# A bank for the value product of the second cross-attention, and the experts' constants and six tiles' gates made before their stage

## The reference

```python
x = x + L0_xattn(ctx, layernorm(x), mask)      # cross-attention, rms-normed heads
x = x + L0_attn(layernorm(x))
x = x + L0_ffn(layernorm(x))                   # small gated low-rank experts
x = x + L1_xattn(layernorm(x), ctx)            # 16 heads of 32, softmax over 257 context rows
x = x + L1_attn(layernorm(x))                  # product of two rotary score matrices, causal
x = x + L1_ffn(layernorm(x))                   # 8 experts of 1024, the best 2 for each token
```

## Time and profile before

| | us |
|---|---|
| median of three timed executions | 1955.49 |
| lowest and highest of them | 1949.67, 1959.02 |
| the profiled execution | 1950.19 |
| its span, first to last instruction | 1948.5 |
| PE busy | 1635.4 (84%) |
| DVE busy | 1301.4 (67%) |
| ACT busy | 957.0 (49%) |
| POOL busy | 616.8 (32%) |

### The profile page before, as it was taken

How to read it: one execution, slowest core, us unless ns; L and a number is a source line. 1 busy time by engine, 2 the same in 40 slices (tenths; PEclk the granted TensorE clock), 3 DMA queues, 4 the chain that set the end, 5 groups by cost and what they waited for, 6 DMA issues and landing times. The chain is left out here.

```text
span 1948.5 us, 43594 instructions
## 1 busy us (share of the span) xinstructions
PE 1635.4 (84%) x15542; PEld 1112.1 (57%) x15542; DVE 1301.4 (67%) x2926; ACT 957.0 (49%) x2169; POOL 616.8 (32%) x730
## 2 busy tenths in 40 slices
PE   6959999999976888399889889759996189989996
PEld 3525555555544666366666666525554077777775
DVE  7858888888855777367777777667775654454441
ACT  5635656565544344255565565533333255565551
POOL 4544545454522110111111111025544123333332
PEclk9989999999987999699999999979998589999998
DMA  5111101011130000101011001330000475665512
GB/s 192 50 49 31 41 30 41 30 41 30 33 124 12 1 2 2 56 27 33 25 32 33 26 31 33 133 133 29 12 12 12 152 223 146 164 186 157 143 31 67
DMA packets 50064, 126.86 MB, mean 65 GB/s; under 512 B 6913, under 2 KB 19425, under 8 KB 49889
## 3 DMA queue, kind: packets, MB, share of 16 engines
q1 hardware_dynamic: 44914, 113.10, 17.9%
q0 software_dynamic: 5008, 11.80, 3.1%
HBM read 111.29 MB, written 15.68 MB: 65 GB/s over the span
## 5 line engine op out<-in xcount | busy, mean ns | idle before, releaser
L106 PE MATMUL e_pGU<-XT,WB 128*128 128x128 f16 x1344 | 233.3, 222 | 18.9 <-issue 9.6
L107 PE MATMUL e_pGU<-XT,WB 128*128 128x128 f16 x1344 | 233.2, 222 | 0.0
L108 PE MATMUL e_pGU<-XT,WB 128*128 128x128 f16 x1344 | 233.2, 222 | 0.0
L2506 DVE SCALAR_TENSOR_TENSOR WB<-w5in,WB 128x1024 f16<-128x1024 f32 x96 | 115.5, 1223 | 85.9 <-ACT WB L2649 85.9
L1639 POOL TENSOR_TENSOR dLT<-dx,dLT 128x768 f16<-128x768 f32 x32 | 52.7, 1647 | 356.6 <-DVE dLT L1663 356.6
L106 PEld LDWEIGHTS e_pGU<-XT,WB 128*128 128x128 f16 x1344 | 134.0, 100 | 24.4 <-issue 22.8
L107 PEld LDWEIGHTS e_pGU<-XT,WB 128*128 128x128 f16 x1344 | 134.0, 100 | 1.5
L108 PEld LDWEIGHTS e_pGU<-XT,WB 128*128 128x128 f16 x1344 | 134.1, 100 | 0.0
L106 PE MATMUL dpK<-dLT,W 128*128 128x256 f16 x384 | 105.9, 276 | 19.0 <-POOL dLT L1639 19.0
L2489 POOL TENSOR_TENSOR XT<-e_mf,XT 128x256 f16<-128x256 f32 x84 | 56.2, 670 | 174.1 <-ACT XT L2663 174.1
L706 POOL TENSOR_TENSOR crn<-css,mhalf 128x8 f32<-128x8 f32 x64 | 106.6, 1666 | 5.3
(11 more groups left out here) (517 smaller groups left out, 5610.4 us busy)
## 6 DMA issues: line engine op xcount, KB each, us to landing
w5in<-in_WE SPq DMA_DIRECT2D x96, 512.0 KB, 4.7
cx<-in_ctx SPq DMA_DIRECT2D x32, 384.0 KB, 3.1
dx<-in_ctxT SPq DMA_DIRECT2D x32, 384.0 KB
w5in<-in_W SPq DMA_DIRECT2D x14, 512.0 KB, 8.6
wpiece<-in_W SPq DMA_DIRECT2D x12, 512.0 KB, 9.3
w3in<-in_W SPq DMA_DIRECT2D x11, 512.0 KB, 9.0
v<-vlat SPq DMA_DIRECT2D x32, 96.0 KB
X<-in_x SPq DMA_DIRECT2D x8, 256.0 KB, 8.2
```

Source lines behind the costliest of these rows:

```text
L106: pe.matmul(out, lh, rh, start=first, stop=False, skip_group_check=shared)
L107: pe.matmul(out, lh, rl, start=False, stop=False, skip_group_check=shared)
L108: return pe.matmul(out, ll, rh, start=False, stop=last, skip_group_check=shared)
L2506: dve.scalar_tensor_tensor(WB[w][:, 1, a], ring[n][:, :], WS, WB[w][:, 0, a], ALU.mult, ALU.subtract)\
```

## The change

It has two parts.

In **cross1** the first half of a batch's values goes into the bank `dpO`, the second into `dpV` (`pVs`). The waits of `values` and `outputs` are rewritten for that. The low half of XT, `out_low`, moves from DVE to POOL, with a new wait of `out_sum` for it. ACT reads the turned probabilities before it gathers the queries.

In **poly** POOL makes the experts' constants at the end of slot 3, SP loads 128 token numbers instead of 1024 and the partition's own number at the start of the stage, and at the end of slot 8 DVE makes the gates of the first six tiles (`EARLY` = 6), with an exponential on ACT. The experts' head makes the gates of the last two tiles, has no constants to make and no numbers to load, and computes its bounds from `count` a little later.

The core of the diff (left out: the declarations of the tiles that now live in both stages, and renamings that follow from them):

```diff
--- before.py
+++ after.py
@@ -1585,6 +1589,7 @@
         pV, pO, pS = ps("dpV", [P, D]), ps("dpO", [P, G, P]), ps("dpS", [P, G, 512])
+        pVs = (pO[:, :, :].rearrange("p g n -> p (g n)"), pV[:, :])
@@ -1643,12 +1648,21 @@
+            def out_low(b):
+                pool.wait_ge(sig["d_ohi"], b + 1)
+                sig.passed(pool, "pool")
+                dst = XT[:, :, :, ds(b * S, S)]
+                pool.tensor_tensor(dst[:, 1, :, :], zo[:, :, :], dst[:, 0, :, :], ALU.subtract).then_inc(sig["d_olo"], 1)
+
...
                     low(b + 1, 1 - u)
-
-            walk(pool, body, lambda: low(0, 0))
+                if prev:
+                    out_low(b - 1)
+
+            sig.begin(pool, "d_olo")
+            walk(pool, body, lambda: low(0, 0), lambda: out_low(B - 1))
@@ -1672,7 +1686,7 @@
                 dve.wait_ge(sig["d_vhi"], q + 1)
-                dve.scalar_tensor_tensor(vb[u][:, i, 1, :], pV[:, :], 1.0 / WS, vb[u][:, i, 0, :], ALU.mult, ALU.subtract)\
+                dve.scalar_tensor_tensor(vb[u][:, i, 1, :], pVs[i], 1.0 / WS, vb[u][:, i, 0, :], ALU.mult, ALU.subtract)\
@@ -1702,16 +1716,12 @@
                 dve.wait_ge(sig["d_o"], b + 1)
+                dve.wait_ge(sig["d_olo"], b + STARTS["d_olo"])
...
                        .then_inc(sig["d_z"], 1)
-
-            def out_low(b):
-                dve.wait_ge(sig["d_ohi"], b + 1)
-                dst = XT[:, :, :, ds(b * S, S)]
-                dve.tensor_tensor(dst[:, 1, :, :], zo[:, :, :], dst[:, 0, :, :], ALU.subtract).then_inc(sig["d_olo"], 1)
@@ -1765,7 +1773,7 @@
                 act.wait_ge(sig["d_v"], q + 1)
-                act.activation(vb[u][:, i, 0, :], pV[:, :], ACT.Copy, scale=1.0 / WS).then_inc(sig["d_vhi"], 1)
+                act.activation(vb[u][:, i, 0, :], pVs[i], ACT.Copy, scale=1.0 / WS).then_inc(sig["d_vhi"], 1)
@@ -1798,10 +1806,11 @@
                 value_high(2 * b, u, 0)
-                gather(b, u)
...
                     probs_high(b - 1, 1)
+                sig.passed(act, "act")
+                gather(b, u)
@@ -1830,10 +1839,15 @@
-            def values(q, u, i):
-                pe.wait_ge(sig["d_vlo"], q + STARTS["d_vlo"])
+            def values(b, u, i):
+                if i == 0:
+                    if not isinstance(b, int) or b:
+                        pe.wait_ge(sig["d_vlo"], 2 * b - 1 + STARTS["d_vlo"])
+                        pe.wait_ge(sig["d_z"], BPT * b - BPT + STARTS["d_z"])
+                else:
+                    pe.wait_ge(sig["d_vlo"], 2 * b + STARTS["d_vlo"])
                 for k in range(XK):
-                    m = product(pe, pV[:, :], hl(LT[u], k, slice(i * P, (i + 1) * P)), hl(Wv, k), k == 0, k == XK - 1)
+                    m = product(pe, pVs[i], hl(LT[u], k, slice(i * P, (i + 1) * P)), hl(Wv, k), k == 0, k == XK - 1)
@@ -1856,9 +1870,8 @@
-            def outputs(b, u):
-                pe.wait_ge(sig["d_vlo"], 2 * b + 2 + STARTS["d_vlo"])
-                pe.wait_ge(sig["d_z"], BPT * b + STARTS["d_z"])
+            def outputs(b, u, nxt=1):
+                pe.wait_ge(sig["d_vlo"], 2 * b + 2 + nxt + STARTS["d_vlo"])
@@ -1876,17 +1889,18 @@
                 keys(b, u)
-                values(2 * b, u, 0)
+                values(b, u, 0)
...
                     turn_probs(b - 1)
-                values(2 * b + 1, u, 1)
+                values(b, u, 1)
...
                 turn_probs(B - 1)
-                outputs(B - 1, (B - 1) % 2)
+                pe.wait_ge(sig["d_z"], BPT * (B - 1) + STARTS["d_z"])
+                outputs(B - 1, (B - 1) % 2, 0)
@@ -2024,6 +2046,17 @@
                     pattern_low(3, q)
+                if s == 3:
+                    tri, before16, ones16 = st["tri"], st["before16"], st["ones16"]
+                    pool.memset(tri[:, :, :], 1.0).then_inc(sig["p_made"], 1)
+                    pool.memset(before16[:, :], 1.0).then_inc(sig["p_made"], 1)
+                    pool.memset(ones16[:, :], 1.0).then_inc(sig["p_made"], 1)
+                    pool.tensor_copy(st["ident16"][:, :], ident[:, :]).then_inc(sig["p_made"], 1)
+                    pool.wait_ge(sig["p_made"], 4)
+                    pool.affine_select(out=tri[:, :, :], in_=tri[:, :, :], compare_op=ALU.is_gt, fill=0.0, base=0,
+                                       pattern=[[1, 8], [-1, 8]], channel_multiplier=0).then_inc(sig["p_made"], 1)
+                    pool.affine_select(out=before16[:, :], in_=before16[:, :], compare_op=ALU.is_gt, fill=0.0, base=0,
+                                       pattern=[[1, P]], channel_multiplier=-1).then_inc(sig["p_made"], 1)
@@ -2148,6 +2181,13 @@
                     logits(r)
+                if r == EARLY - 1:
+                    dve.wait_ge(sig["p_lgc"], EARLY)
+                    dve.wait_ge(sig["p_made"], 6)
+                    for m in (0, 2):
+                        dve.wait_ge(sig[f"p_rr{m}"], NT)
+                    gates(sig, dve, "p_g", 0, LG[:, few, :], st["tri"][:, :, :], gwork)
+                    gates_end(sig, dve, "p_g", 0, st["gate"][:, few, :], gwork)
@@ -2234,6 +2274,9 @@
                         split(n)
+                if r == EARLY - 1:
+                    act.wait_ge(sig["p_g_sh"], 1)
+                    act.activation(gwork["ex"], gwork["sh"], ACT.Exp).then_inc(sig["p_g_ex"], 1)
@@ -2440,8 +2485,6 @@
-            sp.dma_start(flat(slots[:, :, :]), d["slots"].broadcast_to([P, TOK])).then_inc(sig["e_slots"], 16)
-            sp.dma_start(own[:, 0:1], d["slots"][:, 0:P].rearrange("a p -> p a")).then_inc(sig["e_slots"], 16)
@@ -2452,17 +2495,8 @@
             sig.begin(pool, "e_mlo")
-            pool.memset(tri[:, :, :], 1.0).then_inc(sig["e_const"], 1)
-            pool.memset(before16[:, :], 1.0).then_inc(sig["e_const"], 1)
-            pool.memset(ones16[:, :], 1.0).then_inc(sig["e_const"], 1)
-            pool.tensor_copy(ident16[:, :], ident[:, :]).then_inc(sig["e_const"], 1)
             pool.memset(yo[:, :], 0.0).then_inc(sig["e_const"], 1)
-            pool.wait_ge(sig["e_const"], 5)
-
-            pool.affine_select(out=tri[:, :, :], in_=tri[:, :, :], compare_op=ALU.is_gt, fill=0.0, base=0,
-                               pattern=[[1, 8], [-1, 8]], channel_multiplier=0).then_inc(sig["e_const"], 1)
-            pool.affine_select(out=before16[:, :], in_=before16[:, :], compare_op=ALU.is_gt, fill=0.0, base=0,
-                               pattern=[[1, P]], channel_multiplier=-1).then_inc(sig["e_const"], 1)
+            pool.wait_ge(sig["e_const"], 1)
@@ -2508,16 +2542,15 @@
             dve.memset(pY[:, :], 0.0).then_inc(sig["e_no_y"], 1)
-            dve.wait_ge(sig["e_const"], 7)
-            dve.wait_ge(sig["e_slots"], 32)
-            dve.tensor_scalar(bounds[:, :], slots[:, 0, 0:TABLE + 1], float(T), -float(T), ALU.mult, ALU.add).then_inc(sig["e_bounds"], 1)
-            gates(sig, dve, "e_g", 0, LG[:, :, :], tri[:, :, :], work)
+            gates(sig, dve, "e_g", 0, LG[:, late, :], tri[:, :, :], work)
...
             dve.wait_ge(sig["e_g"], 7)
-            dve.tensor_copy(sel16[:, :, :], work["sel"]).then_inc(sig["e_sel16"], 1)
+            dve.tensor_copy(sel16[:, :, :], st["sel"][:, :, :]).then_inc(sig["e_sel16"], 1)
             for i in range(2):
-                dve.tensor_scalar(choice[:, i, :, :], work["rank"], float(i), None, ALU.is_equal).then_inc(sig["e_choice"], 1)
-            gates_end(sig, dve, "e_g", 0, gate[:, :, :], work)
+                dve.tensor_scalar(choice[:, i, :, :], st["rank"][:, :, :], float(i), None, ALU.is_equal).then_inc(sig["e_choice"], 1)
+            dve.tensor_scalar(bounds[:, :], slots[:, 0:TABLE + 1], float(T), -float(T), ALU.mult, ALU.add).then_inc(sig["e_bounds"], 1)
+            gates_end(sig, dve, "e_g", 0, gate[:, late, :], work)
+            dve.wait_ge(sig["e_bounds"], 1)
```

More of the change, by code:

```diff
@@ L43 @@
 E1, INTER = 8, 1024
+EARLY = 6
 IK = INTER // P
@@ L76 @@
 STARTS = {"c0_kh": 1, "c0_vlo": 1, "c0_ktlo": 1, "c0_ss": 1, "c0_olo": 2, "c0_exp": 2, "c0_kt": 1, "c0_pt": 1,
-          "c0_z": 3, "c0_zlo": 1, "d_klo": 1, "d_vlo": 1, "d_z": 1, "d_exp": 1, "d_pt": 1,
+          "c0_z": 3, "c0_zlo": 1, "d_klo": 1, "d_vlo": 1, "d_olo": 1, "d_z": 1, "d_exp": 1, "d_pt": 1,
           "e_mf": 2, "e_mlo": 2, "e_down": 1}
@@ L184, in perceiver @@
         stage(st, cross1)
+        st["tri"], st["count"], st["own"] = sb(ctx, "r_tri", [P, 8, 8]), sb(ctx, "r_count", [P, P]), sb(ctx, "r_own", [P, 2])
+        st["before16"], st["ones16"], st["ident16"] = (sb(ctx, f"r_{n}", [P, P], F16) for n in ("before", "ones", "ident"))
+        st["rank"], st["sel"], st["gate"] = (sb(ctx, f"r_{n}", [P, NT, E1]) for n in ("rank", "sel", "gate"))
         stage(st, poly)
@@ L1919, in poly @@
         xr = two("xr", [P, 2, D], F16)
+        few = slice(0, EARLY)
+        cube = lambda a: a[:, 0:EARLY * 64].rearrange("p (t a b) -> p t a b", a=8, b=8)
+        gwork = {"gt": cube(ra[0]), "eq": cube(rb[0]), "rank": st["rank"][:, few, :], "sel": st["sel"][:, few, :],
```

(19 more changed lines are left out.)

8 lines of the change are left out of this document (3 added, 5 removed).

## The result

| | us |
|---|---|
| before, median of four (lowest, highest) | 1952.58 (1946.37, 1959.02) |
| changed, median of four (lowest, highest) | 1901.47 (1897.51, 1904.64) |
| ratio, 95% interval | 0.974 (0.972 to 0.976) |
| profiled execution of the changed kernel, its span | 1904.64, 1902.9 |

The changed kernel is 51 us faster by the medians and 45.5 by the two profiled executions; the forecast was 47.9. The profiled execution of the changed kernel is the slowest of its four, that of the kernel before is 2.4 us under the median of its four.

A forecast was written before the change was run, and what follows sets the result against it. PE paced cross1, waiting for value bank dpV. Savings 44.0 + 6.0 - 1.8 - 0.3 = 47.9 us gave 1902.3 from the profiled 1950.19 or 1907.6 from the median 1955.49; middle 1905, 8-in-10 range 1897 to 1925.

The forecast's parts named there:

- The pace lost: Cross1 loop: PE's second value product starts 1.39 us later than transpose spacing allows, so the period falls from 13.30 to 11.91.
- the reported idle: Cross1 loop: PE's wait for the value bank as its row reports it, 1.23 us, counted from the last transpose's modelled end.
- The smallest margin: Cross1 loop: DVE finishes subtracting the second half of the probabilities at +10.2, wanted at +10.8; margin 0.6 us.
- The sum of part 1: Cross1: full iterations 41.7, last body 1.0, first body 1.0, tail 0.5 less 0.2; 44.0 us saved in all.
- The 30 full iterations: Cross1 loop: each full iteration saves 1.39 us as PE stops waiting for the value bank, 41.7 us together.
- 1.8 for the gates: Poly drain: early gates on DVE take 4.6 us, idle of 2.79 hides the rest, 1.8 us come on the chain.
- The 0.3 for the clock: Poly drain: PE's longer pause may make its next products run at half clock, at most 0.3 us more.
- The head: Experts' head: 3.86 us for the DMA wait, 2.1 for fewer gates, 0.15 for closing operations, -0.12 for bounds; 6.0 saved.
- The rival that the gather would not move: Experts' head: if the DMA side does not move, 6.0 becomes 0 to 2 us; time 1910 us, chance 0.16.
- the middle that gave 1905: Whole kernel: middle between 1902.3 us, from the profiled execution, and 1907.6 us, from the median of the three timed.
- the slower ring: Cross1 loop: PE's first value product waits for dpO through L1707, ACT and POOL; one us late gives 1977 us; chance 0.02.
- the next wait takes over: Cross1 loop: PE waits for late probabilities instead, some 0.5 to 0.8 us per iteration; gain 28, time 1927 us, chance 0.17.

The follow-up runs named there:

- part 1 alone: Cross1 as changed, with poly and experts as in the kernel before; median 1906.5 us, ratio 0.978 against the kernel before.
- part 2 alone: Poly and experts as changed, with cross1 as in the kernel before; median 1946.8 us, ratio 0.997 against the kernel before.
- either of the other two edits is missing: Changed kernel with ACT gathering queries before reading probabilities, 1938.0 us (period 13.04), or with the low half of XT on DVE, 1907.7 us (period 12.12).
- A bank alone: Changed kernel with ACT gathering first and the low half of XT on DVE, both as before; 1937.9 us, ratio 0.993 against the kernel before.
- an order that gave nothing by itself: Kernel before with poly and experts as changed, and in cross1 only ACT reading probabilities before gathering; 1945.1 us, ratio 0.997.

## Why the prediction was right

- **The period.** Forecast 11.91, measured 11.90. The pace lost (1.39), not the reported idle (1.23), was the right term.
- **The margins.** Forecast against trace: first values read by +8.9 and +8.8; the second half of the probabilities by +10.2 and +10.0; gather by +11.05 and +10.8. The smallest margin was said to be 0.6 and is 0.57, but not of the same thing: the half has 0.8, and 0.57 is that of the 12-row tail behind it, which the forecast left out. That the two figures meet is luck. The kernel with the low half on DVE shows what lies behind the margin: 0.15 beyond it cost PE 0.2.
- **The sum of part 1.** From the first key product to the first split of the next stage: 1264.79 - 826.09 = 438.70 before, 1222.31 - 827.62 = 394.69 after. Saved 44.0, forecast 44.0. Inside it the last body gave 1.15 (forecast 1.0), the first 0.73 (1.0), the tail 0.28 (0.3). The 30 full iterations are the part that the forecast had by its mechanism (41.85 for 41.7). That the whole meets to a tenth is luck: the same stretch took 392.43 in the second profiled execution of the changed kernel and 392.42 with part 1 alone, 46.3 less than before; the 2.3 between lie in the first body and the tail, with the clock.
- **The drain.** Forecast 1.8 for the gates: the residual comes 1.64 later against the logits before it (4.58 for 2.94), the last logits 1.70 later. The 0.3 for the clock had no case for it here: the four us that begin 4 after the logits ran at 0.98, against 0.71 in the kernel before. That belongs to this pair of executions. With part 2 alone the clock there was 0.72 and the drain cost 2.65, 1.0 more than the gates' delay, with the clock still at half 20 us behind the logits. Whether the clock's term comes is not known beforehand.
- **The head.** Forecast 6.0, measured 6.16 to the split and 6.50 to the first product of an expert (30.88 from the memset, 37.38 before). The rival that the gather would not move is refuted by that.
- **What the sum left out.** The polynomial stage was 3.2 longer up to its last logits (2.9 up to the memset of the head), not 2.1: 1.44 lie in slot 8, ahead of the early gates. PE there, the products that follow the output's:

```profile
1424.25 0.61 PE L107 MATMUL pl_bO<-W,pl_yT 128*128 128x512 f16 x1 [0.57 <-DVE pl_yT L2132]
1424.65 0.63 PE L108 MATMUL pl_bO<-W,pl_yT 128*128 128x512 f16 x1
...
1427.54 0.38 PE L109 MATMUL pl_bO<-W,pl_yT 128*128 128x512 f16 x1
1427.75 0.38 PE L107 MATMUL pl_bO<-W,pl_yT 128*128 128x512 f16 x1
```

  Up to 1427.2 they start 0.43 apart, then 0.21: seven products at half clock. Before, the same products ran at full clock. Such things come and go between executions of one kernel (below): in the second profiled execution slot 8 took 24.07. The first key product of cross1 came 1.53 later (827.62 for 826.09), though nothing ahead of it had changed. With these the profiled executions add up: 44.0 in cross1 and 6.2 in the head, less 2.9 in the polynomial stage, 1.5 ahead of cross1 and 0.2 behind the first split, is 45.6. The medians give 51 and not 45.5, since that of the kernel before lies 2.4 above its profiled execution and that of the changed kernel 3.2 below its own.
- **The rivals.** Their times were not counted from one base: from the middle that gave 1905, the first would be 1925 and the slower ring 1980, not 1927 and 1977. That the next wait takes over was the right danger: it is what happens when either of the other two edits is missing (13.04 or 12.12). The slower ring through `dpO` did not show even with POOL's part four times as long. That the head's gain is lost did not come either.

## What to carry to other kernels

When a wait goes, write down for each engine when its next piece is ready and when PE wants it; the smallest margin says which of the accompanying edits carry the gain. A bank alone gave a fifth here, and an order that gave nothing by itself gave most of the rest once the bank was there. Take starts of products for the pace: a stall of 0.2 has no idle time in the rows. Work moved out of a serial head belongs in a gap behind the last thing it needs: here one slot later cost some 0.5 where the earlier one cost 0.9 to 2.7. Before you put a difference of 1 us down to an edit, look at the granted clock of that stretch in both traces.

## What the runs showed of the hardware

- One kernel does not have one time. The changed kernel was profiled twice, with spans of 1902.9 and 1895.3. Cross1 accounts for 2.3 of the 7.6 (1.5 of it in the first body, where the four us that begin 3 after the first key product had a granted clock of 0.64 in the one and 1.00 in the other; 0.7 in the tail), the polynomial stage for 3.9, what lies ahead of cross1 for 1.4. A slot of the polynomial stage took 25.8, 27.5 or 24.1 us by where the clock stood, in kernels whose code is the same there.
- The drain with six early gates took 32.50 to 32.60 six times and 33.49 and 33.56 twice. In the first kind the four us that begin 4 after the logits of tile 5 had a granted clock of 0.92 to 1.00, in the second 0.72 and 0.73. Without early gates it goes the other way: 31.60 at 0.97, 30.84 at 0.71 and 0.73. What decides between them was not found.
- Two of DVE's scalings of 128x256 beside a POOL subtraction of 128x768 ended 0.40 to 0.42 after it in 87 of 90 iterations of three kernels, and took 1.36 to 1.93 by how early they started; with POOL quiet 0.62. DVE's maximum over PSUM took 1.23 beside POOL's subtractions and without them.
- POOL takes 0.43 for a subtraction of 128x128, DVE 0.29 for the same: 1.5 times, where the Trainium skill has about 2 (GPSIMD Engine Reference, section 8, Key points).
